# MLP products of the back pipeline: stationary weights in column halves, two transposes, another order on TensorE

## The reference

```python
def _L1_attn_ref(x, ...):                      # on layernorm(h)
    qkv = einsum(x, W_qkv) + b_qkv             # 16 heads of 4
    k, v = _layernorm(k), _layernorm(v)        # per head
    kv = einsum('bhnd,bhne->bhde', k, v) / HW
    ret = einsum('bhnd,bhde->bhne', q, kv) + x
    return gelu(ret @ W_proj.T + b_proj) + x
def _L1_ffn_ref(x, wr, br, w1, b1, w2, b2):    # on layernorm(h)
    weights = x @ wr + br
    ...                                        # the best 127 of 256 tokens of a sequence
    y = gelu(sel @ w1 + b1) @ w2 + b2          # 64 -> 256 -> 64
    return x with (y * weights) added for the chosen tokens
h = h + _L1_attn_ref(_layernorm(h), ...)
h = h + _L1_ffn_ref(_layernorm(h), ...)
```

## Time and profile before

| | us |
|---|---|
| median of 3 runs | 5161.75 |
| lowest and highest of them | 5156.03, 5164.25 |
| the profiled execution | 5174.49 |
| its span in the trace | 5172.7 |
| the back's steps with all five slots in work | about 4680 to 5100 of the span |

### The profile page before, as it was taken

The page is one execution under the profiler, slowest core; times in us unless marked ns, Lnnn a source line. Parts: engine busy times, 40 slices in busy tenths (PEclk is TensorE's granted clock), DMA queues, the critical chain, the costliest instruction groups (busy, mean ns, idle before and its releaser), DMA issues. The chain is left out here.

```text
span 5172.7 us, 63637 instructions
## 1 busy us (share of the span) xinstructions
PE 3150.6 (61%) x21373; PEld 2430.2 (47%) x21373; DVE 2809.9 (54%) x5797; ACT 2348.0 (45%) x4256; POOL 2221.9 (43%) x2218
## 2 busy tenths in 40 slices
PE   3646663665665665656656656656566566528986
PEld 2445552554454544544544445445445454415664
DVE  8957782454453444544544535445445344478774
ACT  3645564444344444443443444434434444316674
POOL 7866613334344344343343443443434434444420
PEclk8757765777777777777777777777777777756665
DMA  1111101011011011011110110110101101021101
GB/s 58 24 21 21 21 5 44 24 26 30 23 27 30 23 29 28 23 29 28 26 30 23 27 30 23 30 27 24 33 23 27 30 23 27 18 61 52 37 1 33
DMA packets 157531, 145.20 MB, mean 28 GB/s; under 512 B 71240, under 2 KB 133080, under 8 KB 156776
## 3 DMA queue, kind: packets, MB, share of 16 engines
q1 hardware_dynamic: 88656, 109.52, 6.2%
q0 software_dynamic: 68768, 34.45, 5.0%
HBM read 93.00 MB, written 50.82 MB: 28 GB/s over the span
## 5 line engine op out<-in xcount | busy, mean ns | idle before, releaser
L937 PE MATMUL es_pgot<-hash_space,es_pick 128*128 128x256 bf16 x13056 | 1830.0, 287 | 1434.8 <-issue 1429.3
L857 POOL DMA_INDIRECT es_got<-node_table,late x1632 | 1548.2, 949 | 2132.9 <-DVEq L1077 1655.7
L937 PEld LDWEIGHTS es_pgot<-hash_space,es_pick 128*128 128x128 bf16 x13056 | 1295.3, 101 | 1910.8 <-issue 1757.4
L1019 DVE TENSOR_TENSOR es_prod<-es_pgot,es_own 128x512 f32<-128x512 f32 x272 | 187.7, 690 | 1812.2 <-PE es_pgot L937 1630.7
L871 ACT ACTIVATE es_pick<-es_away,consts 128x512 bf16<-128x512 f32 x1088 | 680.0, 711 | 8.4 <-DMA es_away<-sorted_keys 8.1
L293 POOL DMA_INDIRECT fr_ring<-in_emb,fr_rows x384 | 455.8, 1187 | 209.7 <-issue 113.1
L875 ACT ACTIVATE es_pick<-es_pick,consts 128x4096 bf16<-128x4096 bf16 x136 | 503.6, 3703 | 0.9
L894 ACT ACTIVATE ex_hid<-ex_phid,weights 128x256 f32<-128x256 f32 x128 | 53.6, 470 | 695.8 <-PE ex_phid L944 695.5
L1039 DVE TENSOR_TENSOR es_hot<-es_iota,late 128x1024 bf16<-128x1024 f32 x272 | 331.7, 1219 | 29.4 <-DVE es_st L1079 25.7
L1040 DVE TENSOR_TENSOR es_hot<-es_iota,late 128x1024 bf16<-128x1024 f32 x272 | 330.3, 1214 | 0.0
L1021 DVE TENSOR_REDUCE es_got<-es_prod 128x32 f32<-128x512 f32 x272 | 275.9, 1014 | 39.6
(11 more groups left out here) (354 smaller groups left out, 4534.9 us busy)
## 6 DMA issues: line engine op xcount, KB each, us to landing
es_away<-sorted_keys SPq DMA_DIRECT2D x68, 512.0 KB
es_got<-node_table,late POOLq DMA_INDIRECT x1632
edge_states<-es_st SPq DMA_DIRECT2D x68, 384.0 KB
expert_outputs<-ex_y SPq DMA_DIRECT2D x64, 256.0 KB
bk_y<-expert_outputs SPq DMA_DIRECT2D x8, 2048.0 KB
fr_ring<-in_emb,fr_rows POOLq DMA_INDIRECT x384
out_dram<-h SPq DMA_DIRECT2D x4, 1024.0 KB, 5.1
weights<-in_weights SPq DMA_DIRECT2D x1, 2079.0 KB, 13.7
```

The source lines that it names most:

```text
L857: pool.indirect_dma_start(out=got[:, r, k, :], out_offset=None, in_=table_dram, in_offset=bass.IndirectOffsetOnAxis(ap=src[:, n, k:k + 1]. ...
L937: mm = pe.matmul(p_got[:, q, c * 256:c * 256 + 256], pick[:, r, q // 2, k, at * P:at * P + P], parts[:, part, k], start=(k == 0 and part = ...
```

## The change

The second MLP layer is turned round. The weights `m_w2` become the stationary operand, 64 columns at a time, and hid the moving one, 256 tokens at a time. The two sequences b of a slot go to the two halves of the partitions of `p_yt` (which shares a bank with p_hid): four matmuls in place of eight. The bias becomes one column that ACT adds when it copies p_yt to the new tile `yt`; the bias rows on PE and the DVE instructions that prepared them go. Two transposes on PE then bring yt to tokens on partitions in `p_y`, and ACT copies that to xc as before.

The order on PE becomes: ... p_kv, p_kvm, transposes of x3, p_yt (all four products), p_o, transposes of yt, p_q, p_hid and the rest. ACT gets the step yt behind gj; hid now waits for the p_yt products of the slot before and no longer for its p_y; p_hid waits also for yt. Besides, `gate_exp` moves on ACT from the end of step q = 3 to the place between rt and qt, and `gate_scale` on DVE from part 0 to part 1 of q = 3.

```diff
@@ -70,7 +70,7 @@
...
     ("proj_w", 128), ("route_w", SB), ("route_b", 1),
-    ("m_w1", F2), ("m_b1", 2), ("m_w2", 2 * D), ("m_b2", 64),
+    ("m_w1", F2), ("m_b1", 2), ("m_w2", 2 * D), ("m_b2", 1),
 ])
@@ -1286,26 +1286,26 @@
...
         kvm, gj, sq3 = sb("kvm", [P, P]), sb("gj", [P, 2, 2, SB, D]), sb("sq3", [P, ST, D])
-        bias, bias_y, ones = sb("bias", [P, SB * 2 * D + D], BF16), sb("biasy", [P, D], BF16), sb("ones", [P, P], BF16)
+        bias, ones = sb("bias", [P, SB * 2 * D + D], BF16), sb("ones", [P, P], BF16)
         part, rest, exact = (sb(n, [P, SB * 2 * D + D]) for n in ("part", "rest", "exact"))
-        x3, x3t, hid = sb("x3", [P, 2, 2, SB, D]), sb("x3t", [P, T]), sb("hid", [P, 2, SN])
+        x3, x3t, hid, yt = sb("x3", [P, 2, 2, SB, D]), sb("x3t", [P, T]), sb("hid", [P, 2, SN]), sb("yt", [P, T])
         rw, kept = sb("rw", [P, TILES]), sb("kept", [P, TILES])
...
         p_hid = ps("phid", [P, SB, 512])
-        p_xt, p_y = b_xt[:, 0:T], b_xt[:, T:T + ST * D].rearrange("p (t d) -> p t d", d=D)
+        p_xt, p_y, p_yt = b_xt[:, 0:T], b_xt[:, T:], p_hid[:, 0, 0:T]
         p_q, p_prj = b_q[:, 0:T], b_q[:, T:]
...
             sem(n) for n in ("var", "norm", "kvm", "rt", "x2", "xc3", "sum3", "x3", "y", "bias", "dve"))
-        (s_xt, s_sq, s_qt, s_std, s_gj, s_std3, s_x3t, s_hid) = (
-            sem(n) for n in ("xt", "sq", "qt", "std", "gj", "std3", "x3t", "hid"))
-        (s_xt_p, s_kv_p, s_q_p, s_kvm_p, s_o_p, s_prj_p, s_x3_p, s_hid_p, s_y_p, s_rw_p) = (
-            sem(n) for n in ("xtp", "kvp", "qp", "kvmp", "op", "prjp", "x3p", "hidp", "yp", "rwp"))
+        (s_xt, s_sq, s_qt, s_std, s_gj, s_std3, s_x3t, s_hid, s_yt) = (
+            sem(n) for n in ("xt", "sq", "qt", "std", "gj", "std3", "x3t", "hid", "yt"))
+        (s_xt_p, s_kv_p, s_q_p, s_kvm_p, s_o_p, s_prj_p, s_x3_p, s_hid_p, s_yt_p, s_y_p, s_rw_p) = (
+            sem(n) for n in ("xtp", "kvp", "qp", "kvmp", "op", "prjp", "x3p", "hidp", "ytp", "yp", "rwp"))
         s_hx2, s_kv, s_hx3, s_sd = (sem(n) for n in ("hx2", "kv", "hx3", "sd"))
@@ -1422,7 +1422,7 @@
...
                     if last >= 1:
-                        act.wait_ge(s_y_p, last)
+                        act.wait_ge(s_yt_p, last)
                     for m in range(2):
@@ -1440,11 +1440,18 @@
...
                     a.activation(gj[:, joined % 2].rearrange("p two b d -> p (two b d)"), p_prj, ACT.Gelu).then_inc(s_gj, 1)
+                if is_slot(last):
+                    act.wait_ge(s_yt_p, last + 1)
+                    if last >= 1:
+                        act.wait_ge(s_y_p, last)
+                    a.activation(yt[:], p_yt, ACT.Identity, bias=W("m_b2")).then_inc(s_yt, 1)
                 if is_slot(normed):
...
                     a.activation(rt[:, normed % 2], p_o, ACT.Copy).then_inc(s_rt, 1)
+                if q == 3 and g + 2 < GN:
+                    gate_exp(g + 2)
                 if is_slot(new):
@@ -1452,14 +1459,12 @@
...
                     act.wait_ge(s_y_p, last + 1)
-                    a.activation(xc[:, slot(last)], p_y, ACT.Copy).then_inc(s_y, 1)
+                    a.activation(by_half(xc[:, slot(last)]), p_y.rearrange("p (two b d) -> p two b d", two=2, b=SB), ACT.Copy).then_inc(s_y, 1)
                 if is_slot(joined):
...
                         a.activation(sq3[:, t], xc[:, col], ACT.Square, accum_out=rstd3[:, col:col + 1]).then_inc(s_sum3, 1)
-                if q == 3 and g + 2 < GN:
-                    gate_exp(g + 2)
 
@@ -1566,7 +1571,6 @@
...
             exact_rows(do, v, bias[:], both, part[:], rest[:], exact[:], C)
-            exact_rows(do, v, bias_y[:], W("m_b2"), part[:, 0:D], rest[:, 0:D], exact[:, 0:D], C)
             dve.sem_inc(s_bias, 1)
@@ -1578,8 +1582,8 @@
...
                     gate_scores(g + 2)
+                if q == 3 and part == 1 and g + 2 < GN:
                     gate_scale(g + 2)
-                if q == 3 and part == 1 and g + 2 < GN:
                     gate_pick(g + 2, 0)
@@ -1686,12 +1690,6 @@
...
 
-            def outputs(these):
-                for t in these:
-                    for m in range(2):
-                        mm = pe.matmul(p_y[:, t, :], hid[:, m, t * P:t * P + P], W("m_w2")[:, m * D:m * D + D], start=False, stop=(t == ST - 1 and m == 1))
-                return mm
-
             for n in range(STEPS):
@@ -1710,6 +1708,13 @@
...
                     mm.then_inc(s_kv_p, 1)
+                if is_slot(normed):
+                    pe.wait_ge(s_kv, normed + 1)
+                    if normed >= 1:
+                        pe.wait_ge(s_rt, normed)
+                    for half in range(2):
+                        mm = pe.matmul(p_kvm, halves(normed)[:, half, 0:P], halves(normed)[:, half, P:2 * P], start=(half == 0), stop=(half == 1))
+                    mm.then_inc(s_kvm_p, 1)
                 if is_slot(mlp):
@@ -1717,13 +1722,6 @@
...
                     mm.then_inc(s_x3_p, 1)
-                if is_slot(normed):
-                    pe.wait_ge(s_kv, normed + 1)
-                    if normed >= 1:
-                        pe.wait_ge(s_rt, normed)
-                    for half in range(2):
-                        mm = pe.matmul(p_kvm, halves(normed)[:, half, 0:P], halves(normed)[:, half, P:2 * P], start=(half == 0), stop=(half == 1))
-                    mm.then_inc(s_kvm_p, 1)
                 if last == SLOTS - 1:
@@ -1731,18 +1729,23 @@
...
                     pe.wait_ge(s_hid, last * 2 + 2)
-                    if is_slot(new):
-                        pe.wait_ge(s_xt, new + 1)
-                    if last >= 1:
-                        pe.wait_ge(s_y, last)
-                    pe.matmul(p_y.rearrange("p t d -> p (t d)"), ones[0:3], repeat(bias_y[0:3], ST), start=True, stop=False)
-                    outputs((0, 1))
+                    for m in range(2):
+                        for b in range(SB):
+                            mm = pe.matmul(p_yt[b * D:b * D + D], W("m_w2")[:, m * D:m * D + D], hid[:, m, b * T:b * T + T], start=(m == 0), stop=(m == 1))
+                    mm.then_inc(s_yt_p, 1)
                 if is_slot(normed):
...
                 if is_slot(last):
-                    outputs((2, 3)).then_inc(s_y_p, 1)
+                    pe.wait_ge(s_yt, last + 1)
+                    if is_slot(new):
+                        pe.wait_ge(s_xt, new + 1)
+                    if last >= 1:
+                        pe.wait_ge(s_y, last)
+                    for half in range(2):
+                        mm = pe.transpose(p_y[:, half * P:half * P + P], yt[:, half * P:half * P + P], C("ident"))
+                    mm.then_inc(s_y_p, 1)
                 if is_slot(new):
@@ -1751,6 +1754,7 @@
...
                         pe.wait_ge(s_hid, mlp * 2)
+                        pe.wait_ge(s_yt, mlp)
                     for m in range(2):
@@ -1851,7 +1855,7 @@
...
         "m_b1": np.asarray(a["L1_ffn_b1"]).reshape(2, P).T, "m_w2": np.concatenate([a["L1_ffn_w2"][:P], a["L1_ffn_w2"][P:]], 1),
-        "m_b2": row(a["L1_ffn_b2"]),
+        "m_b2": col(*[np.asarray(a["L1_ffn_b2"])] * 2),
     }
```

## The result

The changed kernel takes 5120.98 us (median of 4 runs, 5111.73 to 5124.35) against 5161.86 (5156.03 to 5164.25) for the kernel before. The ratio is 0.9919, with a 95% interval of 0.9904 to 0.9934: about 41 us faster, where 22 were forecast. The profiled execution has a span of 5122.5 us, 50.2 less than before. Cut at X as in the prediction (X is now the end of L1644), the back from the first X to the thirtieth takes 385.70 us (before 420.93), and what follows 69.2 (before 72.7): 38.7 less in the back. The other 11.4 lie ahead of its first X, 9.2 of them ahead of the back's first gates (L1478 at 4607.27, now L1483 at 4598.12). The edge stream itself did not move by more than it does without the change: its L937 matmuls extend over 3690.1 us before and 3686.3 after, and over 3683.6 to 3687.0 in the profiles of the last four variants. So the 38.7 us are what the change explains.

A forecast was written before the change was run, and what follows sets the result against it. Bound: a ring of waits in the back, with PE's own work next. 3.4 us a group over 5 groups gives 17, first and last steps 3, tail 2: 22 us off 5161.75 gives 5140, range 5116 to 5168.

The forecast's parts named there:

- X: Point where the back's steps are cut: the moment DVE has written x3, end of L1640 in the kernel before.
- The ring: Waits round PE, ACT and DVE in one step of the back: closes at 13.4 us at low clock, before 14.87.
- gates' detour: Extra time in some steps of the back: 1.50 us from gate_scale ahead of L1629, 1.53 from gate_exp ahead of L1406.
- the rival that halves run in turn: Rival (a), p_yt on PE: column halves don't overlap, p_yt takes 4.1 us, kernel 5178 us; chance 0.2.
- PE's own work as the bound: PE in a slow step of the back: its work falls from 15.5 to 14.45 us and stops the rest of the gain.
- The sum: Group of four steps in the back: 14.45 + 14.6 + 14.45 + 12.35 = 55.85 us against 59.2, 3.4 saved.
- 12.35: The group's full-clock step in the back: was 12.54 us and sheds only its waits.
- Rival (d): Clock in the back: more of the full clock, about 54 us a group, saving 31 us, kernel 5131; chance 0.18.
- the signs named: Profile after: p_yt about 2.1 us, no PE wait for x3 at low clock, PE nearly full, slow stretches 14.3 to 14.7.
- just covered: gate_scale's 1.0 us on DVE, moved between x3 and the mask of kvm, fits before the mask is needed at X + 3.1.
- forecast 14.6 against 14.9: Step with gate_exp on ACT: 14.6 us with it between rt and qt, 14.9 if left at the end.
- Rival (c): DVE in the back becomes the bound, busy 82% where steps drop to 14 us: half the gain, 5150 us; chance 0.1.

The follow-up runs named there:

- the last four variants: Kernel before with six of eight y products left out (5118.39), p_kvm first (5157.85), x3 first (5148.18); changed kernel with x3 first and p_yt ahead of p_kvm (5090.99 us).
- The second layer alone: Changed kernel with x3 transposes ahead of p_kvm again and gate_scale and gate_exp back in their old places: 3433.28 us, ratio 0.9904 to the kernel before.
- x3 moved first: Changed kernel with x3 computed on DVE ahead of the k and v layernorm and its transposes ahead of p_kvm on PE: 3408.38 us, ratio 0.9831.
- the run beside the variants: Changed kernel without edit, run again on the chip of the first four variants: 3425.04 us against 3467.7 for the kernel before, ratio 0.988.
- the loops swapped: Changed kernel with the loops over m and b of the p_yt products swapped, so two matmuls of one half follow each other: 3424.96 us, ratio 0.9879.

## Why the prediction was right, and where it was off

*The sign and the mechanism.* The ring was the right picture. In the stretch from 4922.78, which has no gates' detour, each link comes out: x3t starts at X + 1.19 (forecast 1.20), gj is done at X + 3.76 (3.77), the transposes of yt start at + 4.18 (4.2), qt starts at + 5.70 (5.9), L1412 ends at + 9.49 (9.68), and the ring closes at 13.26 (13.4). The second layer alone gives 33 of 42 us, and leaving out y products gives 38.

*The price of p_yt.* Forecast 2.15 at the low clock; it is 1.91. The bound from p_hid (2.01 by itself) was the right neighbour, and the rival that halves run in turn is refuted by the 1.91 against 3.60. The estimate from the figure of the Trainium skill ("TensorE: Matmul & The Clock Gate", Part 3) would have been 2.6; the measurement decides for full pairing. Of the drain at a change of tiling mode, which the Trainium skill states ("TensorEngine Tiling (Array Packing)", Key Properties), the trace leaves little room: the four pairs start at 0, 0.48, 0.91 and 1.34 us and p_o at 1.91, so beside four times 0.43 there are some 0.2 for entry and exit together.

*The term that was mis-sized* is PE's own work as the bound, the 14.45 in three steps of four. It rested on the low clock for whole steps. In the changed kernel no step of the group shown is wholly at either level: p_kvm to most of p_q run at 1.2 GHz, p_hid and what follows at 2.4 GHz, and PE then waits 1.44 for kv. The bound that holds is the ring with its 13.3. In the order of the sum the steps are 13.26, 14.05, 13.80 and 12.77 where it had 14.45, 14.6, 14.45 and 12.35 (the 12.77 is the stretch ahead of the other three, at the same place in its group; no row gave the 12.35). One of the 20 steps did keep the low clock throughout, and there PE is nearly full:

```profile
4881.72:4895.95 14.23, 13.69 (x49) 9.01 (x49) 11.56 (x39) 10.80 (x26) 5.37 (x6) 0.50 0.04 4
```

From one L1723 to the next (4882.24 to 4896.72) PE has 14.48 us with a wait of 0.54, so its own work is 13.9 at the low clock. The 14.45 was thus 0.5 too high as well, 0.24 of it by p_yt; another 0.2 is that the 15.5 counted the last matmuls of p_kv by their duration of 2.07 where their start distance is 1.87 (4894.00 to 4895.87). The sum was 55.85 a group; measured are 53.8 in the mean, 2.0 less, so 20 steps save 27.0 us (296.15 to 269.11) and not 17. The first steps and the last save 8.2 where I had put 3, and the tail 3.5 where I had put 2. Together that is 38.7 against 22. Rival (d), with 31 us and 54 a group, was the better number of mine; I had given it 0.18. Of the signs named, PE's wait for x3 is gone as forecast (0.8 us in all, before 35.3), but PE busy for nearly all of a slow step and slow stretches of 14.3 to 14.7 did not come.

*The clock.* I had expected at least as much of the full clock, because PE would be full in three steps of four. More of it came (0.75 against 0.63 over 20 steps), but not for that reason: PE waits in every step. In the kernel before, a rise followed a stretch with no waits. In the changed kernel's step shown it comes at about 4928.2, in p_q, when PE has worked without a wait since 4922.28; the fall comes at about 4935.0, when PE has been idle since 4934.1.

What brings the larger share is in part on record. These are 20 steps of the second layer alone, in the old order, and of the kernel before with the new order alone:

```profile
3027.06:3297.65 270.59, 194.71 (x960) 124.28 (x960) 226.24 (x447) 212.60 (x504) 110.63 (x96) 0.80 0.10 27
4720.76:5012.99 292.23, 251.71 (x1099) 187.44 (x1099) 226.28 (x446) 203.82 (x483) 110.23 (x96) 0.69 0.09 25
```

The new second layer alone has 0.80, the new order alone 0.69 and the two moves of the gates alone 0.71, with fewer y products in the old form 0.65; two profiles of the changed kernel differ by 0.05. So by these profiles, one of each version, it is the new second layer that brings most of the clock, and neither the order nor less work on PE alone. What in it does (the form of the four matmuls, the transposes, where they stand) is open.

*gate_scale.* I took it as just covered. In the step q = 3 the mask ends at 4939.40 and p_o waits 0.35 for it, which was the "some tenths" of the prediction:

```profile
4939.45 1.22 PE L1739 MATMUL bk_pkvm<-bk_qt,bk_kvm 128*128 128x256 f32 x2 [0.35 <-DVE bk_kvm L1648]
```

Its move was not undone by itself, so what it is worth alone is open.

*gate_exp.* The direction was right as far as the run can tell (4.5 us, forecast 14.6 against 14.9, which is 0.3 in six steps, 2 us), the wait of the table load was not. The step with gate_exp takes 14.05, forecast 14.6: 0.8 more than the 13.26 of the step before, where I had put 1.2.

*DVE as the bound.* Rival (c) did not decide the changed kernel, but the step of 13.80 is close to it: DVE is busy for 12.70 of it and its one wait is 0.68 for gj. With x3 moved first DVE is busy for 89%.

## What to carry over

In a pipeline of several engines that hand work round in a ring, add up one turn of the ring from an instruction to its successor a step later, engine by engine, before adding up any engine's work; here it explained the steps before to 0.1 us and the new step without a detour to 0.2; the forecasts of the other three steps of the group were 0.4 to 0.7 off. An engine's own work is a bound only at the clock that it really gets, so carry the sum at both levels, and don't let a saving be capped by a low level that the trace shows for the old order of work. The same swap can be worth 8 us in one version and nothing in the other, so edits to the order have to be measured on the version in which they will stand.

## What the runs showed of the hardware

The same program took 5162 us on one chip and 3466 on another. The edge stream makes nearly all of the difference. Its L937 matmuls have the same median of 273 ns in both, but in the changed kernel's first profile they extend from 844.6 to 4530.9 us, and in the run beside the variants from 781.7 to 2833.1: 1635 us of the 1703 between the two spans, and 63 more lie ahead of them. In the first of these profiles PE is idle ahead of them for 1404 us for nothing that the profile shows ("issue"). In the second it is idle for 16.6, all of it for ACT. The two rows are that group on the pages of two profiles, busy and mean ns, then the idle time ahead:

```profile
L937 PE MATMUL es_pgot<-hash_space,es_pick 128*128 128x256 bf16 x13056 | 1836.0, 288 | 1424.2 <-issue 1403.9
```

```profile
L937 PE MATMUL es_pgot<-hash_space,es_pick 128*128 128x256 bf16 x13056 | 1508.4, 277 | 18.8 <-ACT es_pick L875 18.8
```

(The first is the changed kernel's first profile, the second the run with the second layer alone, on a faster chip.) What in the chips differs is open. The back is nearly the same on both: from the first X to the last, the changed kernel takes 402.6 us on the one, 397.5 on the other, and 403.2 with the loops swapped.

Matmuls on two halves of the array's columns start within 0.02 us of each other even where the program lists both of one half first: four take 1.91 and 1.92 us at 1.2 GHz in the two orders, and 3.60 in one half.
